# All four batches stage by stage: a 73-row stack in the first attention, pipelined feed-forwards, 32 head pairs in one run

## The reference, cut to what matters

```
x = x + tanh(g) * attention0(layernorm(x), context)    # 16 heads of 8, q and k normalised per head
x = x + tanh(g) * ffn0(layernorm(x))                   # shared SwiGLU + LoRA of the top 2 of 8 experts
x = x + tanh(g) * attention1(context, layernorm(x))    # 16 heads of 64, keys: 512 of context + 256 latents
x = x + tanh(g) * ffn1(layernorm(x))                   # the one best of 8 experts, gelu, 128 -> 512 -> 128
```

## Time and profile before

| | |
|---|---|
| time, median of 3 (lowest, highest) | 976.95 us (976.1, 977.69) |
| the profiled execution's own time | 978.69 us |
| its span | 976.5 us, 16529 instructions |
| TensorE busy | 831.4 us (85%) |
| VectorE busy | 629.7 us (64%) |
| ScalarE busy | 380.5 us (39%) |
| GpSimd busy | 307.1 us (31%) |
| mean granted TensorE clock | 0.928 of full |

### The profile page before, as it was taken

How to read it: one execution, slowest core, us unless ns; L and a number is a source line. 1 busy time by engine, 2 the same in 40 slices (tenths; PEclk the granted TensorE clock), 3 DMA queues, 4 the chain that set the end, 5 groups by cost and what they waited for, 6 DMA issues and landing times.

```text
span 976.5 us, 16529 instructions
## 1 busy us (share of the span) xinstructions
PE 831.4 (85%) x6096; PEld 596.8 (61%) x6096; DVE 629.7 (64%) x1149; ACT 380.5 (39%) x677; POOL 307.1 (31%) x271
## 2 busy tenths in 40 slices
PE   3698969997979778999788976999888977899957
PEld 2555756665855556666575665666576556666646
DVE  6774556847976475774897465585599737455543
ACT  2454244341346425333325532534233642434220
POOL 5131025561513013464312101546341301155431
PEclk8699989998989898999798988999989999799979
DMA  7300000003000000001200000000300000000120
GB/s 176 115 2 17 1 0 2 1 1 87 1 8 2 17 1 1 2 1 40 48 3 8 1 17 0 2 1 1 88 0 7 1 1 1 1 2 1 31 56 6
DMA packets 37783, 18.32 MB, mean 19 GB/s; under 512 B 11432, under 2 KB 36408, under 8 KB 37568
## 3 DMA queue, kind: packets, MB, share of 16 engines
q1 hardware_dynamic: 37696, 17.16, 6.9%
HBM read 16.63 MB, written 0.52 MB: 18 GB/s over the span
## 4 chain that ended last, share of the span: by engine, by line
PE 61%; DVE 25%; issue 8%; ACT 3%; POOL 1%; DMA 1%; SPq 1%; DVEq 0%; ACTq 0%; POOLq 0%
PE ps L1248 58%; DVE max_cols L1143 3%; PE ps L1270 2%; DVE rs_t L810 2%; DVE xn L829 1%; DVE area_k L922 1%; DVE area_k L923 1%; DVE area_p L1223 1%; DVE area_p L1231 1%; DVE cn L829 1%; DVE rs_y L816 1%; DVE area_p L1228 1%; DVE area_k L930 1%; PE ps L1344 1%; ACT area_p L718 1%
## 5 line engine op out<-in xcount | busy, mean ns | idle before, releaser
L718 ACT ACTIVATE area_p<-ps 128x512 f32<-128x512 f32 x192 | 104.2, 595 | 157.9 <-PE ps L1248 157.8
L1143 DVE TENSOR_REDUCE max_cols<-ps 128x2 bf16<-128x1536 f32 x64 | 112.8, 1763 | 67.0 <-PE ps L1248 64.1
L553 POOL TENSOR_TENSOR area_p<-area_p 128x512 f32<-128x512 f32 x64 | 80.4, 1278 | 144.0 <-ACT area_p L718 144.0
L1248 PE MATMUL ps<-q_h,keys 64*128 64x256 f32 x768 | 110.7, 326 | 2.2 <-ACT max_row L585 1.6
L1248 PE MATMUL ps<-area_p,area_v 128*64 128x256 f32 x768 | 108.0, 394 | 0.0
L1248 PE MATMUL ps<-area_v 96*128 96x256 bf16 (+1 forms) x384 | 98.1, 323 | 4.2 <-DVE rowmax L994 2.8
L994 DVE TENSOR_REDUCE rowmax<-ps 128x2 f32<-128x1024 f32 x64 | 77.8, 1223 | 25.9 <-PE ps L1248 24.1
L529 POOL TENSOR_TENSOR diag<-negidentb,rowmax 128x256 bf16<-128x256 bf16 x64 | 39.2, 613 | 162.6 <-DVE rowmax L994 158.5
L585 ACT ACTIVATE area_v<-ps 96x768 bf16<-96x768 bf16 (+1 forms) x64 | 53.7, 892 | 88.3 <-PE ps L1248 50.5
L637 ACT ACTIVATE area_p<-ps 128x512 f32<-128x512 f32 x128 | 69.7, 595 | 46.6 <-PE ps L1248 46.3
L1248 PEld LDWEIGHTS ps<-q_h,keys 64*128 64x128 f32 x768 | 74.0, 188 | 22.3 <-issue 9.2
(11 more groups left out here) (234 smaller groups left out, 1625.4 us busy)
## 6 DMA issues: line engine op xcount, KB each, us to landing
area_v<-in_L_ffn_W_dram SPq DMA_DIRECT2D x16, 512.0 KB, 6.3
w<-in_L_ffn_W_dram SPq DMA_DIRECT2D x1, 2048.0 KB
ctx_in<-in_ctx_dram SPq DMA_DIRECT2D x4, 256.0 KB, 2.8
area_p<-in_L_xattn_Wkv_dram SPq DMA_DIRECT2D x1, 1024.0 KB, 7.5
area_v<-in_L_ffn_B_dram SPq DMA_DIRECT2D x9, 64.0 KB
x_in<-in_x_dram SPq DMA_DIRECT2D x4, 128.0 KB, 2.2
area_p<-in_L_xattn_Wq_dram SPq DMA_DIRECT2D x1, 512.0 KB, 8.3
wout<-in_L_xattn_Wout_dram SPq DMA_DIRECT2D x1, 512.0 KB
```

Source lines behind the costliest of these rows:

```text
L553: pool.tensor_tensor(psum_1[:, p % 2, j, :], p1[:, (6 * p + j) % PR1, :], p1[:, (6 * p + 2 + j) % PR1, :], ALU.add).then_inc(g_part.sem, 1)
L718: act.activation(p1[:, n % PR1, :], bank(SCORE_BANK[u][j]), ACT.Exp, scale=SCALE1).then_inc(a_exp1.sem, 1)
L1143: dve.tensor_reduce(max_cols[:, p % 2, :, j * D1], bank(0, 3).rearrange("p (t k) -> p t k", t=TQ), AX, ALU.max).then_inc(d_max1.sem, 1)
L1248: return pe.matmul(o, lhsT, rhs, start=start, stop=stop)
```

## The change

It changes the order from batch by batch to stage by stage, on every engine, written out without loops. x and the context of all batches stay on the chip (`xr`, `ctx_all`).

- **Preparation** of q and k of all four batches comes first. They are kept transposed from the start (centering matrix `cen` in the weights, variance by a matmul with `blk16`), split into three parts, written to DRAM and read back by DMA as the 72 rows of `kq` (`stacked(b)` on SP). Row 73 holds ones on the side of the keys; on the side of the queries it gets the negated maximum of the row by DMA (`maxima_row(q)`).
- **First attention**: 64 heads in 16 quads. Maxima come from float32r operands of 32 rows (`qmr`, `kr`), reduced 512 columns at a time. The products with `diag` are gone; exponentials take 1024 columns. No key or value projections of the second attention lie in it.
- **First feed-forward**: batches overlap; router, common products and layernorm of the next batches stand between the steps of the present one.
- **Second attention**: one run of 32 pairs. Keys, queries and values are projected in the run, three pairs ahead, all through bank 7, whose uses are in one list (`X_USES`); value projections also go through bank 5 (`M_USES`). Maxima are made in three parts in banks 4 and 5. Value products and sums all go to bank 6. GpSimd folds the sums once more, so that `sums1` is half as long.
- **Second feed-forward**: batches overlap; `Gelu` and `Exp` alternate per batch.

The core of the diff, as the new order of the run (TensorE, then VectorE), the new first attention and SP's order:

```diff
+            def scores0(n):
+                ...
+                for k in range(TC):
+                    ins = mm(bank(2 * (n % 2), 2)[:, k * NQ:(k + 1) * NQ], kq[0:SR + 1, b, h, k * P:(k + 1) * P],
+                             kq[0:SR + 1, b, h, NC_:NK])
+            ...
+            def row_max0(q, n):
+                ...
+                if m >= 3:
+                    pe.wait_ge(d_max0.sem, m - 2)
+                at = slice(32 * r, 32 * r + 32)
+                mm(bank(4 + m % 3), qmr[at, b, v, t * P:(t + 1) * P], kr[at, b, :]).then_inc(e_max0.sem, 1)
+            ...
+            def max1(g, part):
+                ...
+                elif part == 2:
+                    pe.wait_ge(d_max1.sem, d_max1.after(g, 2))
+            ...
+            def sums1(g):
+                pe.wait_ge(g_fold.sem, g + 1)
+                for j in range(2):
+                    ins = mm(bank(6)[j * D1:(j + 1) * D1, NQ:2 * NQ], onesf[:, :], fold1[:, g % 2, j, :])
+            ...
+            for g in range(G1 + 1):
+                b, p = divmod(g, NPAIR)
+                if g < G1:
+                    if g + 1 < G1:
+                        max1(g + 1, 2)
+                    scores1(g, 0)
+                    scores1(g, 1)
+                    if g + 1 < G1:
+                        max_row_in(g + 1)
+                        if 1 <= p <= 4:
+                            values_in(b, 1, p - 1)
+                        if p >= 5 and b + 1 < B:
+                            values_in(b + 1, 0, p - 5)
+                    if g + 3 < G1:
+                        project(g + 3, 0)
+                if g >= 1:
+                    values1(g - 1, (0, 1, 2, 3))
+                if g < G1:
+                    scores1(g, 2)
+                    if g + 2 < G1:
+                        max1(g + 2, 0)
+                    if g + 3 < G1:
+                        project(g + 3, 1)
+                if g >= 1:
+                    values1(g - 1, (4, 5))
+                    sums1(g - 1)
+                if g < G1:
+                    if g + 2 < G1:
+                        max1(g + 2, 1)
+                    ...
+            (VectorE)
+            def divide1(g):
+                dve.wait_ge(e_den1.sem, g + 1)
+                ...
+            for g in range(G1):
+                b, p = divmod(g, NPAIR)
+                if g + 1 < G1:
+                    row_max1(g + 1, 2)
+                if g + 3 < G1:
+                    proj_low(g + 3, 0)
+                if g + 2 < G1:
+                    row_max1(g + 2, 0)
+                if g + 3 < G1:
+                    proj_low(g + 3, 1)
+                if g >= 1:
+                    divide1(g - 1)
+                if g + 2 < G1:
+                    row_max1(g + 2, 1)
+                if p == 1 and b >= 1:
+                    residual_c(b - 1)
+                if b + 1 < B:
+                    if p == 0:
+                        context_stats(b + 1)
+                    ...
+                    if p == 2:
+                        context_norm(b + 1)
+                        latents_norm(b + 1)
+                    ...
+            (VectorE, preparation)
+            norm_x(2)
+            norm_x(3)
+            for b in (0, 1):
+                scale0(b)
+            for b in (0, 1):
+                scaled0(b)
+            (SP)
+            tokens(2)
+            for to, of in raw_loads:
+                sp.dma_start(to, of).then_inc(s_raw.sem, 16)
+            tokens(3)
+            ...
+            stacked(0)
+            stacked(1)
+            maxima_row(0)
+            maxima_row(1)
+            stacked(2)
+            stacked(3)
+            for q in range(2, AQ):
+                maxima_row(q)
+            (VectorE, second feed-forward, after select1(i, 0, 1) and summed1(i, 0))
+                if i + 1 < B:
+                    masks1(i + 1)
+                if i + 2 < B:
+                    norm_d(i + 2)
+                select1(i, 1, 0)
+                if i + 1 < B:
+                    masked(i + 1, 0)
+                    masked(i + 1, 1)
```

More of the change, by code:

```diff
@@ L41, with __init__, after, take @@
 class Signal:
[L45 to L49, removed]
+    def __init__(self, sem, per):
+        self.sem, self.per = sem, per
+    def after(self, unit, k):
+        return unit * self.per + k
+class Area:
+    def __init__(self, nc, at, end):
+        self.nc, self.at, self.end = nc, at, end
+    def take(self, name, shape, dtype=F32):
+        n = 2 if dtype == BF16 else 4
+        for d in shape[1:]:
+            n *= d
+        at = (self.at + 31) // 32 * 32
+        self.at = at + n
+        assert self.at <= self.end, (name, self.at, self.end)
+        return self.nc.alloc_sbuf_tensor_at(name, shape, dtype, offset=at)
 def flamingo(nc, t_in, out):
@@ new lines, in _ @@
+            prep_turned(0)
+            prep_turned(1)
+            prep_squares(0)
+            prep_squares(1)
+            prep_final(0)
+            prep_final(1)
+            prep_turned(2)
+            prep_turned(3)
+            prep_middle(0)
+            prep_middle(1)
+            prep_squares(2)
+            prep_squares(3)
+            for n in range(WT_GROUPS - 2):
+                wt_group(n)
+            prep_final(2)
+            prep_final(3)
+            prep_middle(2)
+            prep_middle(3)
@@ new lines, in scale0 @@
+            def scale0(b):
+                k = b % 2
+                dve.wait_ge(e_var.sem, b + 1)
+                vh, y, tmp = (a[:, :] for a in rs_wide)
+                own()
+                then(dve.tensor_scalar(vh, bank(3 * k + 1)[:, 0:TK * H], EPS, -0.5, ALU.add, ALU.mult))
+                if b >= 2:
+                    dve.wait_ge(e_rb.sem, e_rb.after(b - 2, 2))
+                rsqrt(vh, y, tmp, columns=False,
+                      last=rexp[:, k, :, :].rearrange("p t (h d) -> p (t h) d", h=H)).then_inc(d_rs.sem, 1)
@@ new lines, in residual0 @@
+            def residual0(b):
+                x = x_of(b)
+                then(dve.scalar_tensor_tensor(out=x, in0=wide(bproj0[:, :], TQ, P), scalar=G_X0, in1=x,
+                                              op0=ALU.mult, op1=ALU.add))
+                dve.wait_ge(e_proj.sem, b + 1)
+                dve.scalar_tensor_tensor(out=x, in0=halves(bank(7)[:, 0:NQ]), scalar=G_X0, in1=x, op0=ALU.mult,
+                                         op1=ALU.add).then_inc(d_xA.sem, 1)
+            for q in range(2):
+                for n in range(8):
+                    row_max0(q, n)
@@ L1185, in batch, with norm_d, route1 @@
+            divide1(G1 - 1)
+            def norm_d(i):
+                dve.wait_ge(x_free.sem, X_AT["wout", i] + 1)
+                if i >= 2:
+                    dve.wait_ge(e_xTD.sem, i - 1)
+                layernorm(xnD[:, i % 2, :, :], x_of(i)).then_inc(d_xnD.sem, 1)
+            def route1(i):
+                dve.wait_ge(e_lgD.sem, i + 1)
+                own()
+                then(dve.tensor_scalar(probT[0:E, :], bank(6)[0:E, NQ:2 * NQ], gate1_b[:, :], None, ALU.add))
                 then(dve.tensor_reduce(sm[:, 0:1], probT[0:E, :], AX, ALU.max))
```

2494 lines of the change are left out of this document (1310 added, 1184 removed).

## The result

The changed kernel takes 1093.0 us (median of 4 runs, 1089.2 to 1094.3) against 977.2 us (976.1 to 977.7): 1.118 times as long, 95% interval 1.115 to 1.121. The forecast was 1056 us, range 985 to 1115, slower with a chance of 0.84. So the sign and the range held and the point was 37 us short. The profiled execution took 1089.2 us, its span is 1087.5. Its mean granted clock is 0.833 of full, against 0.928 before: that is 181 us of lost TensorE time against 70, though not all of it lies on the path.

What follows compares the result with a forecast made beforehand. It took TensorE's throughput to bound the head pairs and TensorE-VectorE handoffs the rest. Stages of 90, 136, 101, 37, 476, 48 (clock) and 168 us gave a span of 1056; forecast 1056 us, range 985 to 1115.

Steps and rivals of the forecast that it cites:

- Prologue: Start until the first scores, with all four batches' operands prepared first: 90 us, bounds 72 and 100.
- First attention: 64 heads in 16 quads, bound by TensorE at 7.0 us a quad: 136 us in all, bounds 115 and 145.
- The second failed step: Start of the first attention: two stacks on SP, 10 us each, delay exp number 4 and quad 2, costing 11 us.
- First feed-forward: Pipelined over batches, VectorE setting a period of 23 us: 101 us, bounds 88 and 110.
- Head: Start of the second attention, now once with nothing beside it: 37 us, bounds 28 and 42.
- Run of pairs: 32 pairs of the second attention, TensorE waiting behind sums, division and reduction: period 13.8 us, 476 us at full clock.
- Clock in the pairs: Pair run: TensorE's new wait lowers the clock, 1.5 us a pair, 48 us in all, bounds 0 and 109.
- Second feed-forward: Last stage, pipelined, with 16 us to the first expert matmul: 168 us, bounds 145 and 180.
- Rival B: Pair run: wait behind the division is covered, 11.3 us a pair at TensorE's throughput; total 908 us, chance 0.13.
- Rival A: Pair run: waits as forecast but the clock holds; total 1008 us, chance 0.2.
- Rival C: Clock falls in every pair for longer, and VectorE's small operations meet GpSimd's more; total 1126 us, chance 0.14.
- Rival D: Shared bank or DMA round trips of stacks and maxima bind, 16 x 2 us more; total 1088 us, chance 0.05.

Runs made afterwards that it cites:

- with 72 rows: Changed kernel with the first attention's maxima computed from the stacks in place (72 rows, bf16) instead of 32-row slices: 1068.7 us.
- The 32-row and full-height versions: The changed kernel itself (maxima matmuls on 32 rows), 1093.0 us, and the same with those of the first attention on all 128 rows, 1058.7 us.
- the other order: Changed kernel with SyncE issuing the whole stacks of batches 2 and 3 ahead of the first two rows of maxima: 1109.5 us.
- the run with the filled wait: Changed kernel with 16 added full-height matmuls of 256 columns per pair in TensorE's wait behind the sums, into a free bank: 1074.5 us.
- the reordered runs: Changed kernel with VectorE's pair order altered: division one place later, 1102.1 us; order by who waits, 1043.6; that plus norms taken apart, 1016.8.

## Why the prediction was right or wrong, step by step

1. **Prologue: right** (91.2 for 90), and its steps too: VectorE gets x of batch 3 at 28.3 us (28 taken), the last of the first scalings ends at 42 (43), and the tanh that VectorE waits for comes at 81 (78).
2. **First attention: wrong, by 61 us; the failed step is "TensorE per quad: ... Sum 7.0 ... So TensorE bounds it: 16 x 7.0 = 112".** The sum of durations was near: plain quads at full speed take 7.35 us with 72 rows and 7.6 with 128, 0.7 to 1.1 of it a wait for VectorE, and 10.99 less the 3.4 lost to the clock is 7.6 with the turning. What was missing is the clock: no term for it where TensorE is busy. The 32-row and full-height versions show 34 us for it. The second failed step is "these are 16 issues and a write-and-read wait each (10 us each) ... 11 us": a stack takes SyncE 15 to 21 us, quad 2's scores start 46 us after quad 0's, and the other order, which the step implies, costs 16 us. Spreading the reads gives 23 back.
3. **First feed-forward: mechanism right, size short** (111.5 for 101, bounds 88 to 110). `residual_b` of batches 0 to 2 ends at periods of 26.4 and 27.6 us instead of 23. 20 of its us are cold, for which this part had no term.
4. **Head: right in time** (39.8, within 28 to 42), though the terms given add up to 35 (5.5, 3.8, 4, 16.8 and 5) and not to the 37 that was taken.
5. **Run of pairs: right in mechanism, and the term that decides.** The cycle is the one described, 3.4 us against 3.5. The period is 13.16 against 13.8, just under the bounds: 20 us less over the run. The extras of a batch are near 12 us in the run with the filled wait (five pairs of 16.1, 18.5, 15.9, 13.9 and 13.6 us less five of 13.16), 36 for 30.
6. **Clock in the pairs: right in kind, the size too large.** I took 1.5 us in each pair. It fell 19 times over 32 pairs; laid beside the run with the filled wait, the 31 intervals are 20.3 us longer (455.8 against 435.5), 0.65 a pair. That is 28 of the 55 us by which the stage was overestimated, and the period is 20 more. The reading "3.4 to 6.8 us" of a cold stretch was short as well: the fall at 283 in the kernel before lasts 6.8 us and not only the 3.4 of the window shown, and the longest there last 13.7.
7. **Second feed-forward: 178.5 for 168**, inside its bounds of 145 to 180. The later batches take 37.5 and 40.4 us (975.0 and 1015.4 less their forerunners), as forecast. The head, to the mask products ahead of the first expert matmul (909.0 to 937.6), takes 28.6 instead of 16: while GpSimd splits the down weights, VectorE's small steps for the second norm stretch from 0.16 to 2.3 us, 8 us in all. The clock is down there too, from 909.4 to 933.3; what that costs was not measured.

Rival B had the wait covered because "other work fills the 3.5 us"; the reordered runs show that it can be, but not in the changed kernel. Rival A fell with the clock of 0.91. Rival C fell in its main part, since the clock dropped 19 times and not in each of 32 pairs; its second part, VectorE's small operations beside GpSimd's, came true in the last stage. Rival D named the round trips over DRAM and put 2 us on each quad; the stacks' issues and landings cost 32 us once, at the start. That 55 us too many in the pairs stood against 61 too few in the first attention is luck.

## What to carry to other kernels

When a wait is to be removed by moving an instruction, list what is second in that engine's queue and who waits for it: moving the division by one place moved the wait, moving it by who waits gave 49 us. Put long strided DMA issues between the short ones that a chain needs, not ahead of them. And when a full-height matmul is replaced by row tiles that don't run side by side, count the clock: here the same 512-column matmuls cost 34 us more on 32 rows, with their changes of tiling, than on 128.

## What the runs showed of the hardware that was not expected

- TensorE fell to 1.2 GHz eleven times out of stretches in which it was busy 90 to 98%, when the work was matmuls of 32 rows beside values of 32 columns; with the same count at 128 rows it held 2.4 GHz, at 85% busy.
- In the pairs each of 19 falls stood behind a wait of 2.1 to 5.7 us; with no wait over 1.5 us there was none.
- A 32-row matmul of 512 columns with one of 128 rows ahead of it in the same bank, twice over, takes 1.69 us at full speed; grouped by kind and in two banks 1.33.
- VectorE's operations on two columns stretch beside GpSimd's subtractions: the pair at L876 from 0.36 to 4.57 us. The chain of waits at the start of the last stage of the changed kernel (start, length); GpSimd splits the down weights from 918.0 to 927.3:

```profile
918.11 2.30 DVE rs_y L887
920.44 4.57 DVE rs_t L876 x2
925.03 2.28 DVE rs_y L887
927.33 0.36 DVE rs_t L876 x2
```

- Twelve reads for one stack hold SyncE for 10.3 us by their issue alone, 0.3 to 1.8 us each.
